# Attention scores of four tokens per product, softmax weights turned by TensorE, NF4 work moved between stages, and FFN chunks in groups of 4, 4, 1 and 2

## What is computed

```python
q = (x @ wq.T + bq).reshape(B, S, 32, 16)       # k and v alike
scores = einsum('bshd,bstd->bsht', q, k) / 4    # 32 x 32 per token
context = einsum('bsht,bstd->bshd', softmax(scores), v)
x = layernorm(x + context)
dq = nf4_quant_dequant(w)                       # w1, w2 (1376 x 512), w3 (512 x 1376)
h = silu(x @ dq1.T) * (x @ dq2.T)
out = layernorm(x + h @ dq3.T)
```

## Time and profile before

| | us |
|---|---|
| median of three runs (755.1 to 756.2) | 755.46 |
| the profiled execution | 755.57 |
| its span, first to last instruction | 753.8 |
| TensorE busy | 680.4 (90%) |
| VectorE busy | 590.4 (78%) |
| ScalarE busy | 475.8 (63%) |
| POOL busy | 108.7 (14%) |

### The profile page before, as it was taken

The page is one execution under the profiler, slowest core; times in us unless marked ns, Lnnn a source line. Parts: engine busy times, 40 slices in busy tenths (PEclk is TensorE's granted clock), DMA queues, the critical chain, the costliest instruction groups (busy, mean ns, idle before and its releaser), DMA issues.

```text
span 753.8 us, 14539 instructions
## 1 busy us (share of the span) xinstructions
PE 680.4 (90%) x5818; PEld 556.7 (74%) x5818; DVE 590.4 (78%) x810; ACT 475.8 (63%) x652; POOL 108.7 (14%) x98
## 2 busy tenths in 40 slices
PE   4969999998986968758999999999999999999983
PEld 3858878787875857647888788888887888888761
DVE  2458999899997997967978998998778885544386
ACT  2559989886845647458638788886657673342134
POOL 0105411231101010101101121111110201000022
PEclk9989999999997988968999999999999999999995
DMA  9934237765684686728023542013313101330447
GB/s 213 231 113 155 98 125 190 175 175 132 108 126 79 178 145 160 198 83 311 1 113 140 194 116 85 17 56 103 140 33 130 63 1 30 138 117 13 158 121 167
DMA packets 132850, 92.90 MB, mean 123 GB/s; under 512 B 90256, under 2 KB 111760, under 8 KB 131504
## 3 DMA queue, kind: packets, MB, share of 16 engines
q1 hardware_dynamic: 131648, 89.88, 43.3%
q10 hardware_dynamic: 1136, 2.10, 1.2%
HBM read 58.07 MB, written 33.88 MB: 122 GB/s over the span
## 4 chain that ended last, share of the span: by engine, by line
PE 54%; DVE 24%; issue 9%; DMA 5%; ACT 5%; POOL 1%; SPq 0%; DVEq 0%; POOLq 0%; ACTq 0%
DVE nf_acc L1188 12%; PE ps_s L950 8%; PE ps_s L952 8%; PE ps_s L951 8%; PE ps_p L950 7%; PE ps_p L952 7%; PE ps_p L951 7%; DMA queries_keys<-qk_p 2%; PE ps_s L1033 2%; ACT nf_y L785 2%; DVE prob L1217 2%; DVE smax L1213 2%; DMA wst<-in_L_attn_wk 2%; PE ps_p L1059 1%; DVE y_tmp L1236 1%
## 5 line engine op out<-in xcount | busy, mean ns | idle before, releaser
L1188 DVE SCALAR_TENSOR_TENSOR nf_acc<-nf_y,nf_acc 128x1024 f32<-128x1024 f32 (+4 forms) x266 | 316.7, 1191 | 35.5 <-ACT nf_y L785 23.6
L785 ACT ACTIVATE nf_y<-nf_w,bound_b 128x1024 f32<-128x1024 f32 (+4 forms) x285 | 286.6, 1048 | 3.7 <-DVE nf_acc L1188 3.3
L705 POOL TENSOR_TENSOR nf_w<-nf_w,nf_rec 128x1024 f32<-128x1024 f32 (+4 forms) x19 | 44.4, 2336 | 308.5 <-DVE nf_rec L1172 308.5
L1322 DVE TENSOR_TENSOR silu<-silu,ps_s 128x512 f32<-128x512 f32 (+1 forms) x44 | 30.1, 685 | 74.5 <-PE ps_s L952 74.4
L950 PE MATMUL ps_p<-x_hl,w_hl 128*128 128x512 f32 x192 | 78.1, 407 | 8.9 <-DVE w_hl L1206 6.3
L950 PE MATMUL ps_s<-x_hl,f_ha 128*128 128x512 f32 x192 | 75.0, 391 | 1.6 <-DVE f_la L1206 1.6
L952 PE MATMUL ps_p<-x_hl,w_hl 128*128 128x512 f32 x192 | 76.3, 397 | 0.0
L951 PE MATMUL ps_p<-x_hl,w_hl 128*128 128x512 f32 x192 | 76.2, 397 | 0.0
L932 ACT ACTIVATE hid_hl<-silu 128x512 fp32r<-128x512 f32 (+1 forms) x44 | 27.8, 632 | 76.1 <-DVE silu L1322 76.1
L952 PE MATMUL ps_s<-x_hl,f_la 128*128 128x512 f32 x192 | 74.8, 390 | 0.0
L951 PE MATMUL ps_s<-x_hl,f_ha 128*128 128x512 f32 x192 | 74.8, 390 | 0.0
(11 more groups left out here) (108 smaller groups left out, 1187.4 us busy)
## 6 DMA issues: line engine op xcount, KB each, us to landing
x_hl<-x_parts SPq DMA_DIRECT2D x10, 2048.0 KB, 8.3
queries_keys<-qk_p SPq DMA_DIRECT2D x32, 256.0 KB, 3.4
x_parts<-x_st SPq DMA_DIRECT2D x16, 512.0 KB, 3.6
nf_w<-in_L_ffn_w SPq DMA_DIRECT2D x24, 256.0 KB, 3.1
dequantised<-nf_acc SPq DMA_DIRECT2D x10, 512.0 KB, 2.7
v_blocks<-v_t SPq DMA_DIRECT2D x16, 256.0 KB, 3.2
k_st<-queries_keys SPq DMA_DIRECT2D x64, 64.0 KB, 3.8
v_bd<-v_blocks SPq DMA_DIRECT2D x32, 128.0 KB, 3.5
```

The source lines that it names most:

```text
L705: pool.tensor_tensor(v, v, nf_rec[0:p, 0:w // QBLOCK].unsqueeze(2).to_broadcast([p, w // QBLOCK, QBLOCK]), ALU.mult).then_inc(s_nnorm, 1)
L785: act.activation(nf_y[0:p, at % NY, 0:w], nf_w[0:p, u % 2, 0:w], ACT.Identity, bias=bound_b[0:p, i:i + 1], scale=STEEP).then_inc(s_ny, 1)
L1188: dve.scalar_tensor_tensor(out=acc, in0=y, scalar=float(NF4[i + 1]), in1=acc, op0=ALU.min, op1=ALU.max).then_inc(s_nacc, 1)
L1322: dve.tensor_tensor(h, h, ps_s[0:rows, 1], ALU.mult).then_inc(s_hid, 1)
```

## The change

Scores: a product has four tokens. The queries of four tokens (64 rows by 32 heads) are the weights, 128 columns of block-diagonal keys move, 16 products a group; the row half `r` alternates and the four column tiles are gone through. The key buffers double. The maximum and the subtraction are as before. The exponentials are then turned by TensorE, four 128x128 transposes into the PSUM bank that held the group's scores (`swap`, now on TensorE), and ScalarE copies them out to `probT` (`keys_first`). So `scores(G)` waits for the copy of group G - 2. `LV_A` gives two levels to most groups (49 in all instead of 39), `LV_F` keeps five a step for longer and needs 153. The FFN groups are 4, 4, 1 and 2 chunks; in the last one both chunks of w1 and w2 stand ahead of w3 among the units, and the last w3 unit is turned in step 37, the step after the group's first. Buffers move within SBUF, so the values' buffers are cleared and first loaded later (from product 44 on), and the load of x1 for block 1 waits for the last `values`.

```diff
-    J2, TN = 2, TI // 2
+    R2, TN = 2, TI // 2
-    GROUPS = [range(0, 4), range(4, 8), range(8, 10), range(10, NJ)]
+    GROUPS = [range(0, 4), range(4, 8), range(8, 9), range(9, NJ)]
-        first = len(js) if g == 0 else 1
+        first = len(js) if g in (0, len(GROUPS) - 1) else 1
-    FIRST_LOADS = {3 * KC * (NBK - 1) + at: what for at, what in ((-7, "keys 0"), (-5, "values 0"), (-3, "keys 1"),
-                                                                  (1, "queries 0"), (3, "queries 1"))}
+    FIRST_LOADS = {3 * KC * (NBK - 1) + at: what for at, what in ((-7, "keys 0"), (-3, "keys 1"), (1, "queries 0"),
+                                                                  (3, "queries 1"), (10, "values 0"))}
-    LV_A = [2, 1] * (GG // 2)
+    LV_A = [2] * GG
     for b in range(NBK - 1):
         LV_A[8 * b + 10:8 * b + 15] = [1, 1, 1, 1, 1]
-    LV_F = [(1, 2)] * 2 + [(1, 1)] * 2 + [(1, 0), (1, 2)] + [(2, 3)] * 20 + [(2, 2)] * 13
+    LV_F = [(1, 2)] * 2 + [(1, 1)] * 2 + [(1, 0), (1, 2)] + [(2, 3)] * 33
...
         def load_side(eng, i, hb, a):
-            (q, j), (b, e) = divmod(a, J2), divmod(hb, 2)
-            rows, t0 = slice(32 * q + D * j, 32 * q + D * j + D), TB * e + TI * q + TN * j
+            (r, q), (b, e) = divmod(a, Q4), divmod(hb, 2)
+            rows, t0 = slice(D * a, D * a + D), TB * e + TI * q + TN * r
...
         load_x1, n == 1:
-                    sp.wait_ge(s_probT, GG)
+                    sp.wait_ge(s_pv, GG)
...
             def clear(slot):
-                if slot == 1:
-                    pool.wait_ge(s_proj, VALUES_FREE)
+                pool.wait_ge(s_proj, (VALUES_FREE, 3 * KC * NBK)[slot])
-                if tau == 3 * KC:
+                if tau == VALUES_FREE:
                     clear(0)
                     ones(0)
...
         ScalarE:
+            def keys_first(G):
+                act.wait_ge(s_swap, G + 1)
+                wait(act, s_pv, G - 1)
+                act.activation(probT[:, G % 2], ps_s[:, G % 2].rearrange("p (u k) -> p u k", u=Q4), ACT.Copy
+                               ).then_inc(s_probT, 1)
             for G in range(GG):
                 steep(LV_A[G])
+                if G:
+                    keys_first(G - 1)
...
         TensorE:
             def scores(G):
-                wait(pe, s_ssub, G - 1)
-                for i in range(GI // J2):
-                    for q in range(Q4):
-                        rows, n = slice(32 * q, 32 * q + 32), GI // J2 * g + i
-                        t = pe.matmul(ps_s[32 * q:32 * q + 32, G % 2, J2 * H * i:J2 * H * (i + 1)],
-                                      q_st[hb % 2][rows, :, n],
-                                      k_st[hb % 2][rows, :, :, n].rearrange("d j h -> d (j h)"), start=True, stop=True)
+                wait(pe, s_probT, G - 1)
+                for i in range(GI):
+                    u, c = divmod(i, 4)
+                    r, n = c % 2, TN // NG * g + 2 * u + c // 2
+                    rows = slice(TI * r, TI * r + TI)
+                    t = pe.matmul(ps_s[32 * c:32 * c + 32, G % 2, P * u:P * u + P], q_st[hb % 2][rows, :, n],
+                                  k_st[hb % 2][rows, :, :, n].rearrange("d q h -> d (q h)"), start=True, stop=True)
                 t.then_inc(s_score, 1)
+            def swap(G):
+                pe.wait_ge(s_exp, G + 1)
+                for u in range(Q4):
+                    t = pe.transpose(ps_s[:, G % 2, P * u:P * u + P],
+                                     prob[:, G % 2, 4 * u:4 * u + 4].rearrange("p q h -> p (q h)"), ident[:])
+                t.then_inc(s_swap, 1)
             for G in range(GG):
                 scores(G)
+                if G:
+                    swap(G - 1)
                 if G >= 2:
                     values(G - 2)
...
         VectorE:
             def shift(G):
                 dve.wait_ge(s_smax, G + 1)
+                wait(dve, s_swap, G - 1)
-            def swap(G):
-                dve.wait_ge(s_exp, G + 1)
-                wait(dve, s_pv, G - 1)
-                dve.transpose(probT[:, G % 2].rearrange("p i h -> p (i h)"),
-                              prob[:, G % 2].rearrange("p i h -> p (i h)")).then_inc(s_probT, 1)
             for G in range(GG):
                 highest(G)
-                if G:
-                    swap(G - 1)
                 shift(G)
```

54 lines of the change are left out of this document (29 added, 25 removed).

## The result

The changed kernel is slower: 767.07 us, the median of four runs (766.48 to 768.70), against 755.52 us for the kernel before on the same chip. The ratio is 1.0158, with a 95% interval from 1.0142 to 1.0174. The profiled execution took 767.09 us with a span of 765.2 us, 11.4 more than the 753.8 of before. The forecast was 745.2 us, 21.9 us too low, and the upper end of the range 755.

The account below looks back on a forecast made before the run. It took VectorE to bound the attention and TensorE the FFN up to 712.3 us, but not the end. Attention -4.7 and end -5.6 made -10.3 us from 755.46: 745.2 us, range 735 to 755.

Parts of the forecast that it names:

- Scores, taken at 1.2 us a group: Attention, TensorE: 32 score records instead of 64 take 1.2 us a group, bringing its plain group to 3.4 us.
- Ten levels: Attention, VectorE: ten more levels cost 11.6 us against 20.2 saved by the transposes; their absence in the FFN earns nothing.
- (a): Groups G11 to G13, their like, and three before a norm: VectorE works back to back, saves 0.62 each, -7.4 us.
- (b): Plain groups of the later attention that get a second level: +0.7 us over both blocks.
- (c): Behind a norm VectorE waits for ScalarE; second level and copy delay the context copy, partly covered: +0.2 us in all.
- (d): After the last norm the same delay goes straight into the start of the FFN: +1.6 us.
- Memsets and value loads, at nothing: Before and in early attention: later value clearing and loads stay hidden, at worst 1 us; doubled key memset lies beside products.
- The end: Last FFN group with two chunks: last drain starts 9.5 us earlier; after give-backs of 1.0, 2.4 and 0.5, -5.6 us.
- Step 37 at +2.4: FFN: turning the last group's second w3 unit where the first down product waits for both copies costs +2.4 us.
- rival (4): Attention: the two row halves don't overlap, so scores take 1.9 to 3.8 us a group; 769 us, chance 0.10.
- rival 2: ScalarE takes VectorE's place so fully that the attention gains nothing, only the end does; 750 us, chance 0.17.
- rival 3: The attention loses what the end earns, with the last group's reload late; 755 us, chance 0.08.

Follow-up runs that it names:

- after_levels_back: The changed kernel with the levels per group of before (ten fewer in the attention, made up in the FFN): 760.32 us, ratio 1.0053.
- reload_first: The changed kernel with SyncE issuing each FFN step's reloads ahead of that step's loads of new units: 762.83 us, ratio 1.0089.
- fewer_beside_drain: Changed kernel with later key clearing, reloads ahead of loads, last units turned in steps 32 to 35, and 3 levels, not 5, in FFN step 8: 757.22 us.
- contiguous_keys: The changed kernel with each score product's 128 moving columns read from neighbouring numbers of the key tile (output wrong): 764.08 us, ratio 1.0116.
- full_rows: The changed kernel with every score product over all 128 rows instead of a half of 64 (output wrong): 765.88 us, ratio 1.0140.

## Why the prediction was wrong, point by point

**Scores, taken at 1.2 us a group: 2.0.** This is the step that failed first. From 64 records that took 2.07 us at the lower clock as at the higher the prediction concluded "0.032 is the spacing of instructions and not array time". Not array time was right. Spacing was not: it was the strided read, 0.5 ns a column, and doubled with the columns to 0.062. Without a stride 128 columns do come 0.035 us apart and a group takes 1.11, near the 1.2. TensorE's plain group is 4.23 us, not 3.4, and is the bound in plain groups, which the forecast had given to ScalarE: in after_levels_back seven maxima in a row come 4.22 or 4.23 us apart.

**Turning at 0.5 and copy at 0.5: 0.58 and 0.59.** Right. **ScalarE's group at 3.85:** right, 3.83, once the scores were cheap.

**Ten levels: the second step that failed.** VectorE's 3.43 for a group with two levels left out a unit's maximum, denominator and reciprocal, which are on VectorE once in 15 levels (1.21 us for the maximum alone), and used 1.13 a level where two levels of a wide unit take 2.59. The first eleven groups rose by 5.85 us where the forecast's 41.4 makes +1.1 (its +0.2 counts the earlier first scores with them, 0.9 there, 0.8 by its own 2.0 less 1.2): 4.19 remain with cheap scores (44.53), and -2.0 with cheap scores and old levels (38.32). That "the ten levels leave a TensorE-bound stage, so their absence earns nothing" was right: with the reload's wait mended, steps 0 to 32 take 281.2 us, and 280.9 before with ten levels more.

**The other 21 groups.** (a) The groups with context turns gained more than was said: the three stretches from the 12th to the 15th, the 20th to the 23rd and the 28th to the 31st maximum together 7.0 us, where 9 x 0.62 = 5.6 were forecast; the three groups behind them gained 1.3, forecast 1.9. (b) The plain ones lost 3.7 us (18th to 20th, 26th to 28th) where 0.7 was forecast; with half of the score columns they lose 0.85, so the miss is the scores again. (c) Behind a norm (15th to 18th and 23rd to 26th maximum) +3.2 and +0.2, forecast +0.2 for both together: the first of them is SyncE's queue and the second level, as above. The second was luck: with the same attention that stretch takes 17.97 us in the changed kernel and up to 19.91 in others, where ScalarE waits 2.15 us for the x1 store there too. The prediction walked the three engines' queues and not SyncE's. (d) +1.2 from the last maximum to the first FFN product (24.48 us against 23.29), forecast +1.6: right.

**Memsets and value loads, at nothing.** Right for the values: no TensorE wait in the attention is for them. Wrong for the keys: that the doubled key memset lies beside products looked at TensorE only, and the memset held VectorE, for whose copies TensorE waits: 0.9 us more, and 1.6 of slow products behind it, +2.0 in this execution.

**Steps 8 to 16, not in the sum at all, +9.3; with steps 16 to 32, +4.6.** The prediction asked what TensorE's 363 us cover, but not where the starts of units would fall once ten levels are done earlier. They moved from steps 8 and 11 to step 9, where SyncE has a reload to issue and VectorE a drain. reload_first gives 4.3 of the 4.6 back. fewer_beside_drain takes 2.7 from step 8, but only 0.2 from steps 0 to 32.

**The end.** Forecast -9.5 + 1.0 behind step 38, measured -8.6: right. Step 37 at +2.4: the wait is 2.66, right, but 13.15 us against 8.16 make +5.0, since slow products follow the gap; where the clock held, 11.5 make +3.4. The x1 loads at +0.5: no wait. Left out: each w3 unit of the two-chunk group is turned in two parts where the one-chunk group needed one, and one of the gate and up units moves from step 28 into this stretch.

**The rivals.** The measured 767 is near rival (4)'s 769, but its mechanism is refuted by contiguous_keys: the row halves overlap. Its condition, scores above 2.6 us a group, was not met either. That the attention gains nothing (rival 2) and that the last group pays back (rival 3) both came true in part, and each with a mechanism it did not name. None of its three signs of being wrong came in full: score records were 62 ns apart (sign: 80), G4 to G9 3.92 to 4.23 us apart (sign: 4.2), and TensorE did not wait for x1. They were set too wide for a miss of this size.

**The sum.** Of the 21.7 us by which the span exceeds the forecast's 743.5, the attention has 10.9, steps 0 to 32 4.6, steps 32 to 38 4.4 and the start 2.9; the way into the FFN gives 1.0 back.

## What to carry to other kernels

A spacing of records that does not follow the clock may be a read: look at the distance between the numbers that a product moves before taking the spacing for a price per instruction. When an edit moves work between stages, write down for every queue, the DMA queue's own among them, which step now holds the start of a unit, and what stands behind the wait it brings. A stretch between two marks can shrink because work has moved over a mark, so add up the stretches beside it before calling it a gain. And when two bounds lie close together, price the edit by both at once: here each alone was worth 2.4 and 4.8 us, both together 12.7.

## What the hardware showed that I had not expected

Products whose moving numbers lie 144 bytes apart take 1.98 us for 32 records of 128 columns at a granted clock of 0.50 and of 1.00, and 1.11 us with neighbouring numbers at full clock: the clock was no part of their price. A clearing on POOL that touches nothing of VectorE's stretched a VectorE instruction from 0.69 to 1.61 us. And the same wait of 2.66 us on TensorE was followed by products at a granted clock of 0.57 in the changed kernel and of 1.00 in reload_first (13.15 and 11.5 us for the step). At 100 us the same happens: a wait of 2.37 us in the changed kernel is followed by a granted clock of 0.50, one of 2.34 in full_rows by 1.00. No run here shows what decides between the two. Whether a layout that keeps four tokens' keys side by side could be loaded without new cost was not tried; with it the new attention would have one of its two bounds less.
